# A gated delta rule layer: the triangular inverse started from 16x16 blocks that pass through memory, with a new order of steps

## The reference, cut to what matters

```python
q = silu(conv(x @ Wq)); k = silu(conv(x @ Wk)) * DK**-0.5; v = silu(conv(x @ Wv))   # causal, 4 taps
alpha = sigmoid(x @ Wa + ba); beta = sigmoid(x @ Wb + bb)
def step(S, inps):                      # scanned over the 2048 positions
    qt, kt, vt, at, bt = inps
    err = S @ kt - vt
    S = at * S - bt * outer(err, kt)
    return S, S @ qt
o = layernorm(o) * ln_w + ln_b
out = (o * sigmoid(x @ Wg)) @ Wo
```

## Time and profile before

| | |
|---|---|
| median of 3 runs | 3923.45 us |
| profiled execution, own time | 3925.09 us |
| its span (first to last instruction) | 3923.5 us |
| mean granted TensorE clock | 0.986 |
| TensorE busy | 3769.9 us, 96% |
| VectorE busy | 2704.0 us, 69% |
| ScalarE busy | 2204.4 us, 56% |
| GpSimd busy | 1281.8 us, 33% |
| DMA | 275.67 MB, 70 GB/s |

### The profile page before, as it was taken

The page is one execution under the profiler, slowest core; times in us unless marked ns, Lnnn a source line. Parts: engine busy times, 40 slices in busy tenths (PEclk is TensorE's granted clock), DMA queues, the critical chain, the costliest instruction groups (busy, mean ns, idle before and its releaser), DMA issues. The chain is left out here.

```text
span 3923.5 us, 119759 instructions
## 1 busy us (share of the span) xinstructions
PE 3769.9 (96%) x41088; PEld 3063.9 (78%) x41088; DVE 2704.0 (69%) x6942; ACT 2204.4 (56%) x6016; POOL 1281.8 (33%) x2594
## 2 busy tenths in 40 slices
PE   7999889999999999999999999999999999987999
PEld 5777668888888888888788888888888888866887
DVE  3444458878788777788777778777887878863222
ACT  3433356666666666666666666666666666652111
POOL 3434433333333333333333333333333333320000
PEclk9999989999999999999999999999999999988999
DMA  3343341111111211111321111111111211215443
GB/s 134 111 147 141 117 128 45 51 45 47 45 45 48 55 50 46 45 48 48 90 88 46 45 48 48 45 48 45 47 49 45 48 45 45 50 24 163 144 146 109
DMA packets 371786, 275.67 MB, mean 70 GB/s; under 512 B 153457, under 2 KB 284529, under 8 KB 369361
## 3 DMA queue, kind: packets, MB, share of 16 engines
q1 hardware_dynamic: 368848, 261.29, 23.5%
q0 software_dynamic: 2560, 8.39, 0.6%
HBM read 209.85 MB, written 59.77 MB: 69 GB/s over the span
## 5 line engine op out<-in xcount | busy, mean ns | idle before, releaser
L1084 DVE SCALAR_TENSOR_TENSOR conv<-bank,tap,conv 128x512 f32<-128x512 f32 x1152 | 857.6, 744 | 79.3 <-ACT conv L1233 56.4
L1295 PE MATMUL bank<-hx_hi,w_hi 128*128 128x512 f32 x2048 | 874.2, 427 | 35.2 <-POOL w_lo L913 24.0
L1295 PE MATMUL bank<-hx_hi,w_lo 128*128 128x512 f32 x2048 | 899.4, 439 | 0.0
L1295 PE MATMUL bank<-hx_lo,w_hi 128*128 128x512 f32 x2048 | 881.5, 430 | 0.0
L1295 PEld LDWEIGHTS bank<-hx_hi,w_hi 128*128 128x128 f32 x2048 | 391.3, 191 | 71.7 <-issue 49.0
L1295 PEld LDWEIGHTS bank<-hx_lo,w_hi 128*128 128x128 f32 x2048 | 389.0, 190 | 50.7
L931 POOL TENSOR_TENSOR prods<-Lb,Tc 128x28 f32<-128x28 f32 (+6 forms) x896 | 203.6, 227 | 683.6 <-ACT Lb L1219 621.2
L1295 PEld LDWEIGHTS bank<-hx_hi,w_lo 128*128 128x128 f32 x2048 | 389.9, 190 | 40.1
L965 POOL TENSOR_TENSOR oG<-oT,gT 128x512 f32<-128x512 f32 x128 | 163.7, 1279 | 721.7 <-ACT oT L1254 721.7
L1037 DVE SCALAR_TENSOR_TENSOR S<-S,gamma,bank 128x128 f32<-128x128 f32 x480 | 163.6, 341 | 203.9 <-PE bank L1376 191.7
L1207 ACT ACTIVATE Wc<-bank 128x128 f32<-128x128 f32 x512 | 141.4, 276 | 242.4 <-PE bank L1367 242.3
(11 more groups left out here) (156 smaller groups left out, 8836.3 us busy)
## 6 DMA issues: line engine op xcount, KB each, us to landing
gamma<-gamma_d SPq DMA_DIRECT2D x128, 258.0 KB, 3.4
alpha<-alpha_d SPq DMA_DIRECT2D x128, 256.0 KB, 3.1
oT_d<-oG SPq DMA_DIRECT2D x128, 256.0 KB, 2.4
o_raw<-oT_d SPq DMA_DIRECT2D x32, 1024.0 KB, 6.8
gu_raw<-in_gate_up SPq DMA_DIRECT2D x17, 1408.0 KB, 6.3
dn_raw<-in_down SPq DMA_DIRECT2D x17, 512.0 KB, 4.5
x_in<-in_x SPq DMA_DIRECT2D x8, 1024.0 KB, 9.3
w_raw<-in_Wk SPq DMA_DIRECT2D x32, 256.0 KB, 3.6
```

Of the source, the lines that this page charges most:

```text
L1084: dve.scalar_tensor_tensor(out=conv[i][:, to], in0=PJ[PJ_OF[(g + 3) % 4][i]][:], scalar=tap[:, i, j + 1:j + 2], in1=conv[i][:, to], op0=AL ...
L1295: last = pe.matmul(dst, a[:, i, k], b[:, k, cols], start=(j == 0), stop=(j == 3 * KC - 1))
```

## The change

- SB goes from 8 to 16: GpSimd inverts 16x16 diagonal blocks, 15 columns, so 30 instructions in place of 14. One doubling level of 32x32-block products (16 to 32) is left.
- The blocks reach GpSimd in another way. ScalarE copies four 32-partition diagonal blocks from LT into diag, GpSimd masks them and adds the two halves (Lc), SP stores Lc twice to a buffer in DRAM (32 KB each), waits, and loads it as Lb with one broadcast of 16 rows of 4 KB to 128 partitions (512 KB). The spreading matmul, Lx, the four products, the reduction and the copy of Lb go.
- TensorE visits the blocks twice a turn, in steps 20 and 1: each visit holds 16 products of 32x32, 8 between 32-row quarters and 4 of 64x64, of three successive groups.
- The stages are further apart: projections run one group further ahead, kT and gT have 6 buffers, qT, vT, decay and TT 3. There is a fourth ramp turn, and the last head has no projection at all. The loop body is three heads.
- For the first chunk of a head (S is zero) the two matmuls with S and R are left out, for the last chunk the one that would update S, and one k transpose in the third group.
- All tables of steps are new. On VectorE, T16 (the transpose of the solved blocks) and LT are both in step 18, T16 first. On SP, the stores and the load stand behind alpha, ahead of the weights and of oG's store. On GpSimd the next weight cut of a head's last turn stands in step 36, the start of the solve in step 37.
- At the start of the stage ScalarE cuts the first weights before it waits for the masks.

The diff, cut to its core:

```diff
-SB = 8
+SB = 16
 TB = 32
-LEVELS = [8, 16]
+NB = P // SB
 STEPS = 38
-
-CHAIN = {0: 0, 5: 1, 8: 2, 11: 3, 13: 4, 17: 5, 20: 6, 24: 7, 26: 8, 29: 9, 32: 10, 34: 11}
+UNROLL = 3
+
+CHAIN = {1: 0, 6: 1, 8: 2, 11: 3, 15: 4, 18: 5, 19: 6, 22: 7, 23: 8, 26: 9, 30: 10, 36: 11}
...
-A_AT, KT_AT, VT_AT, ON_TURN_AT, L_AT, BASE_AT = 1, 2, 11, 18, 24, 30
-VISIT_AT = {9: 0, 15: 1, 28: 2, 34: 3}
-SOLVE_AT = {34: (0, 2), 36: (2, 4), 0: (4, 6), 2: (6, 7)}
-T8P_AT, POW_AT, QG_AT, OG_AT = 4, 8, 17, 20
-AT_AT, K_AT, T8_AT, TN64_AT, DECAY_AT, LT_AT, DIAG_AT, LX_AT = 2, 3, 3, 21, 16, 25, 26, 28
-BN_AT, AGGR_AT, ON_AT = 1, 6, 9
-YB_AT = {11: 0, 28: 1}
-TT_AT = {19: 0, 31: 1}
-CONV_AT = {12: (0, 0), 14: (0, 1), 16: (0, 2), 20: (1, 0), 22: (1, 1), 25: (1, 2), 29: (2, 0), 33: (2, 1), 37: (2, 2)}
-VSILU_AT, GATE_AT, DIAGB_AT, VROWS_AT, KSILU_AT, QSILU_AT, OT_AT, LB_AT = 4, 5, 16, 11, 16, 25, 21, 28
-PLACE_AT = {8: (0, 1), 7: (2, 3)}
-TN_PLACE_AT = 23
-LATE_COPY = {8: 0, 17: 1, 27: 2, 37: 3}
-O_AT = {14: 0, 23: 1, 34: 2, 2: 3}
-TAP_AT = {11: 0, 20: 1, 25: 2}
-CUT_AT = {(0, 17): 0, (0, 21): 1, (0, 36): 2, (1, 4): 3}
-LATE_PER = 4
+A_AT, KT_AT, VT_AT, ON_TURN_AT, L_AT = 5, 2, 8, 22, 18
+VISIT_AT = {20: 0, 1: 1}
+SOLVE_AT = {37: (0, 1), 0: (1, 4), 1: (4, 6), 4: (6, 9), 7: (9, 11), 9: (11, 14), 11: (14, 15)}
+T16P_AT, POW_AT, QG_AT, OG_AT, DIAG_AT, LC_AT = 11, 15, 28, 29, 18, 17
+AT_AT, K_AT, T16_AT, TN64_AT, DECAY_AT, LT_AT = 6, 4, 18, 16, 7, 18
+BN_AT, AGGR_AT, ON_AT = 4, 5, 19
+YB_AT, TT_AT = 35, 0
+CONV_AT = {8: (0, 0), 9: (0, 1), 12: (0, 2), 19: (1, 0), 22: (1, 1), 23: (1, 2), 32: (2, 0), 33: (2, 1), 35: (2, 2)}
+VSILU_AT, GATE_AT, DIAGB_AT, VROWS_AT, KSILU_AT, QSILU_AT, OT_AT = 1, 16, 0, 14, 15, 30, 29
+PLACE_AT = {30: (0, 1), 7: (2, 3)}
+TN_PLACE_AT = 6
+MT32_AT, TT64_AT, MT64_AT, TT128_AT = 21, 4, 27, 6
+O_AT = {16: 0, 28: 1, 29: 2, 1: 3}
+TAP_AT = {14: 0, 17: 1, 28: 2}
+CUT_AT = {(3, 20): 0, (3, 23): 1, (3, 36): 2, (0, 18): 3}
 SOLVE_PER = 2 * (SB - 1)
-BUILT = 9 + 3 * len(LEVELS)
+BUILT = 12
...
-        diag = sb("diag", [P, G, TB])
-        Lc = sb("Lc", [P, G, SB])
-        Lx = sb("Lx", [P, G, SB, SB])
-        Lb = sb("Lb", [P, G, SB, SB])
+        Lb = sb("Lb", [P, SB, G, SB])
         prods = sb("prods", [P, G, SB])
+        Lc = prods
+        diag = same[:].rearrange("p (c t) -> p c t", t=TB)
...
+            turn(eng, -1, 0, 8, False, False, False, False, True, False)
+            turn(eng, -1, 1, 9, False, False, False, True, True, False)
+            turn(eng, -1, 2, 10, False, False, True, True, True, False)
+            turn(eng, -1, 3, 11, False, True, True, True, True, False)
             for g in range(GROUPS):
-                turn(eng, 0, g, True, True, True, True, g > 0)
-            with nc.Fori(1, NH - 1, engines=bass.OrderedEngineSet([eng.engine]), hint_back_edge=True) as hh:
-                for g in range(GROUPS):
-                    turn(eng, hh, g, True, True, True, True, True)
+                turn(eng, 0, g, g, True, True, True, True, True, g > 0)
+            with nc.Fori(1, NH - 1, UNROLL, engines=bass.OrderedEngineSet([eng.engine]), hint_back_edge=True) as h3:
+                for j in range(UNROLL):
+                    for g in range(GROUPS):
+                        turn(eng, h3 + j, g, (4 + 4 * j + g) % 12, True, True, True, True, True, True)
             for g in range(GROUPS):
-                turn(eng, NH - 1, g, True, g < 3, g < 2, g < 1, True)
-            turn(eng, NH, 0, False, False, False, False, True)
+                turn(eng, NH - 1, g, 4 + g, True, g < 3, g < 2, g < 1, False, True)
+            turn(eng, NH, 0, 8, False, False, False, False, False, True)
...
+            def spread(hh, g, d):
+                at = counter(hh, g)
+                for half in range(2):
+                    if half == 0:
+                        sp.wait_ge(lc_done, at(1, d + 1))
+                    sp.dma_start(base_d[:, half], Lc[:].rearrange("p c t -> p (c t)")).then_inc(base_stored, 16)
+                sp.wait_ge(base_stored, at(32, d + 1))
+                row = SB * G * SB
+                sp.dma_start(Lb[:].rearrange("p i c t -> p (i c t)"),
+                             bass.AP(base_d.tensor, 0, [[row, P // 8], [0, 8], [1, row]])).then_inc(base_loaded, 16)
...
+                if not (isinstance(hh, int) and hh == NH - 1):
+                    spread(hh, g, 4)
+                if g == 1 and after_next:
...
+                    if proj and s == LC_AT:
+
+                        pool.wait_ge(diag_done, at(4, 5))
+                        pool.tensor_tensor(diag, diag, same_c[:].rearrange("p (c t) -> p c t", c=1)
+                                           .to_broadcast([P, G, TB]), ALU.mult).then_inc(masked, 1)
+                        wait(pool, solve_done, at(SOLVE_PER, 4))
+                        pool.wait_ge(masked, at(1, 5))
+                        pool.tensor_tensor(Lc[:], diag[:, :, 0:SB], diag[:, :, SB:TB], ALU.add).then_inc(lc_done, 1)
+                    if inv and s == T16P_AT:
...
+                    if inv and s == T16_AT:
+
+                        dve.wait_ge(t16_done, at(1, 4))
+                        wait(dve, mid_done, at(2, 1, 1))
+                        wait(dve, tn_placed, at(2, 2))
+                        dve.transpose(Tnb[:, par], TTb[:, par]).then_inc(tn_done, 1)
...
+                    if proj and s == DIAG_AT:
+
+                        act.wait_ge(lt_done, at(1, 5))
+                        wait(act, masked, at(1, 4))
+                        for q in range(P // TB):
+                            act.activation(diag[quad(q)], LT[quad(q), g, :, quad(q)], ACT.Copy).then_inc(diag_done, 1)
...
-                    if proj and s == LB_AT:
-
-                        act.wait_ge(spread_done, at(1, 4))
-                        wait(act, t8_done, at(1, 3))
-                        act.activation(Lb[:].rearrange("p c t i -> p (c t i)"), TR[:, 0:G * SB * SB], ACT.Copy)\
-                           .then_inc(lb_done, 1)
...
                 def visit(v):
 
-                    if inv:
+                    if inv if v == 0 else mid:
...
+                    if mid if v == 0 else late:
...
+                    if late if v == 0 else chain:
...
+                    first, final = g == 0 and c == 0, g == 3 and c == 3
+                    if r == 0 and not first:
...
+                        if not first:
+                            pe.matmul(w[:, 3 * D:], q_gamma[:, cur, chunk(c)], S[:], start=True, stop=False)
+                        last = pe.matmul(w[:, 3 * D:], AT[:, cur, c], Wc[:], start=first, stop=True)
+                        if not final:
+                            last = pe.matmul(w[:, 2 * D:3 * D], k_rows[:, cur, c], Wc[:], start=True, stop=True)
+                        last.then_inc(chain_done, 1)
...
-                    if proj and s == BASE_AT:
-
-                        pe.wait_ge(lx_done, at(1, 4))
-                        pe.matmul(TR[:, 0:G * SB * SB], same[:], Lx[:].rearrange("p c t i -> p (c t i)"),
-                                  start=True, stop=True).then_inc(spread_done, 1)
```

More of the change, by code:

```diff
@@ L881, in _ @@
             n = 0
[L882 to L883 removed]
+            for tile in (none[:], TT[:], Tn64[:], decay[:, :, :, 0:1]):
                 pool.memset(tile, 0.0).then_inc(built, 1)
                 n += 1
+            pool.memset(oT[:, 0:P], 0.0).then_inc(built, 1)
             pool.memset(same[:], 1.0).then_inc(built, 1)
+            n += 2
+            pool.wait_ge(built, n)
+            part = oT[:, 0:P].rearrange("p (q r) -> p q r", r=TB)[:, :, 0:SB]
+            pool.memset(part, 1.0).then_inc(built, 1)
             n += 1
[L888 removed]
             blocks = same[:].rearrange("p (q r) -> p q r", r=SB)
@@ L894, in _ @@
                 pool.wait_ge(built, n)
+            for base, step, mult in ((-SB, -TB, 1), (TB - 1, TB, -1)):
+                pool.affine_select(out=part, in_=part, compare_op=ALU.is_ge, fill=0.0, base=base,
+                                   pattern=[[step, P // TB], [0, SB]], channel_multiplier=mult).then_inc(built, 1)
+                n += 1
+                pool.wait_ge(built, n)
             pool.wait_ge(sel_built, G)
@@ L916, in _, with turn @@
                 cut_low(i, i + 1)
-            pool.wait_ge(compact_built, 1 + len(LEVELS))
-            def turn(pool, hh, g, chain, late, inv, proj, ln):
+            pool.wait_ge(compact_built, 2)
+            def turn(pool, hh, g, n, chain, late, mid, inv, proj, ln):
                 at = counter(hh, g)
@@ new lines, in turn @@
+                    if late and s == MT64_AT:
+                        act.wait_ge(late_done, at(2, 1, 1))
+                        for odd in range(2):
+                            rows = slice(0, 64) if odd else slice(64, 128)
+                            act.activation(MT[64:128, odd::2], w64[rows], ACT.Copy).then_inc(mt64_done, 1)
+                    if chain and s == TT128_AT:
+                        act.wait_ge(late_done, at(2, 1))
```

(28 more changed lines are left out.)

462 lines of the change are left out of this document (205 added, 257 removed).

## The result

The changed kernel takes 3767.07 us (median of 4 runs, 3762.55 to 3769.11), the one before 3923.95 (4 runs beside it): ratio 0.9595, 95% interval 0.9579 to 0.9612, 157 us less. The prediction was 3711 us with a range of 3642 to 3835: right in sign and range, and 56 us too low.

A forecast was written before the change was run, and what follows sets the result against it. The prediction took TensorE as the bound before, and TensorE (21.4 us a turn) and the inverse's loop (20.6) as nearly level after. 1034.1 us plus 124 turns of 21.6 gave 3712.5, as median 3711, range 3642 to 3835.

The forecast's parts named there:

- The bound: Heads stage before the change: TensorE, busy 98%, sets the steady turn of 23.44 us; only its work or waits count.
- Parts 1 to 3: TensorE's small-block visits (0.94), spreading matmul (0.62), skipped chain steps (0.17): 1.73 to 2.2 us a turn saved, 2.0 taken.
- TensorE then needs 21.4 us a turn.: TensorE's turn in the heads stage after the savings: 21.4 us, between 21.2 and 21.7.
- Part 5: New loop through the inverse (T16, LT, stores, load, solve): 20.6 us, bounds 19.9 and 24.5; turn taken as 21.6.
- Scans against the solve: VectorE's four decay scans taking turns with GpSimd's solve would add 1.3 us, a loop of 21.9; scans above 0.42 speak for it.
- Part 6: Loop body of three heads, ten back edges for thirty: 16 us or 0.13 a turn saved, or nothing; inside the 21.6.
- Part 7: Start and end of the stage: +21 us (0 to 35) for the ramp, +18 for the fourth turn without projection.
- The sum: Whole kernel: T = 1034.1 + 124x us, x the turn; 21.6 gives 3712.5, the median of runs 3711.
- A: Inverse's loop alone decides, scans and solve in turn, late T16 on top: turn 22.4, 3812 us; chance 0.2.
- B: TensorE alone decides and its upper saving holds: turn 21.1, 3650 us; chance 0.12.
- C: Round trip through memory at its upper bounds, 9.8 us for 5.9: loop 24.5, 4072 us, slower than before; chance 0.07.
- D: New TensorE waits between second and third chunk's steps, now one apart, eat most savings: turn 23.0, 3886 us; chance 0.06.

The follow-up runs named there:

- no trip: Changed kernel without the stores, the 512 KB load and the wait for it, the solve working on zeros: 3720.18 us, ratio 0.948.
- load in two: Changed kernel with the broadcast load split into 128 KB and 384 KB, each with its own wait (also called the split kernel): 3745.09 us, ratio 0.9542.
- the last version: Changed kernel with third weight cut on VectorE, load in two pieces, other steps for the cuts and two ramp x loads issued later: 3685.95 us, ratio 0.9395.

## Why the prediction was right or wrong, step by step

- **The bound.** Right in the main: TensorE set the turn before and sets it after, but for two intervals of four in which the loop holds it by 0.5 and 0.1 us.
- **Parts 1 to 3, 2.0 us off TensorE.** Right in sum: the turns away from the head's change went from 23.14 to 21.15 (no trip, load in two), 1.99 less. The new visits take 1039.97 - 1038.64 - 0.31 = 1.02 us (0.95 predicted). The spread is worth 0.63, or 0.57 beside the unrolled loop (0.62). The skips 0.10 to 0.14 (0.17). The 0.31 that I took for a plain step is the one right behind other matmuls; behind another projection matmul it is 0.23 or 0.24 at most places of the same stretch. That makes each visit and the spread 0.08 dearer, so the sum of the parts would have been some 1.97 and not 1.73, an estimate from those rows. But the pieces don't add up as they were worked out: the passes of the dropped level, priced at 0.76, gave 0.1 to 0.2, and 0.29 on the mean, while the chain stood where it was.
- **"TensorE then needs 21.4 us a turn."** This is the term that was off. It took 2.0 from 23.44, a mean with 0.28 us of waits at the back edge in it, and so carried these over. After, the waits around the head's change are 0.60 a turn (21.75 - 21.15). Worked out from the split kernel's timeline over 27 heads, each between two matmul starts less the usual step: T16 behind the weight cut 0.73 us a head, two late Wc of 0.74 and 0.54, and before or at the first product of the new chain 0.63 for the copy of TT in 18 heads or 0.44 for issue in the nine with the back edge. These make 2.6 us a head, 0.65 a turn. Taken as 21.75, TensorE alone would have given T = 3731.
- **Part 5, the loop.** Half right. Its parts, means of the trace after (the 0.49 is that of the second interval, which waits for nothing else): T16 and the way to LT 0.26 at the least, LT to mask 2.10, mask and sum 0.86, to the load's issue 2.6, load 4.7, solve 10.2, T16P to T16 0.49: 21.2 us without a weight cut, where I had 20.3. The stores were 0.5 too low (the second starts 0.68 us behind the first, where I had 0.4) and the load 0.8 (4.6 to land, 3.8 predicted). So loop and TensorE are level, and what the trip costs the turn is 0.16 us, close to the 0.2 that I added. The weight cut I spread over the head as 0.3 of loop; it is a wait of TensorE's, 0.73 us a head or 0.18 a turn, trip or no trip, and moving it gave 0.5 to 0.6 a head.
- **Scans against the solve.** The solve took 10.2 us to T16P's start, and the sum without any taking of turns was 9.9. In the timeline a product beside a scan took 0.36 us between neighbours of 0.26 and 0.28. Over the trace, worked out by size, a solve instruction beside a scan is 0.02 us longer than one without, 0.1 us a turn. The scans have a median of 0.41 us (0.399 before); the one of 1.2 us is the very first, at 500.8, ahead of any solve, and no other took over 0.55. By the prediction's own sign, over 0.42, 213 of the 512 scans speak for the lock, but the size does not: 0.1 to 0.3 us a turn and not 1.3. By the rule of the Trainium skill, "SBUF — State Buffer", section "SBUF: two separate sides", the loop would have been 21.9. The trace does not agree: its whole solve is 0.3 us over the sum without it.

```profile
L1113 DVE TENSOR_TENSOR_SCAN decay<-alpha,diag_b x512: 383/410/1215, 500.8 to 3287.3; 128x128 f32<-128x128 f32 x171
```

- **Part 6.** Right: 0.14 us a turn in the kernel before by the table and 0.11 by the total (0.13 predicted), and 0.41 beside the turn without the spreading matmul.
- **Part 7.** 15 us too low. The constant is 3765.86 - 124 x 21.905 = 1050 where I had 1034.1. Three loops of the ramp take 72.4 us (30.6, 20.9, 20.9), not 60.9: the first waits in SyncE's queue. The rest, 4 us, is at the end. Two more misses of 7 to 8 us cancel: the first scan starts 8 us earlier than before (500.8), and the ways from it to the first LT and from the last loop to the chain are longer than the 3 and 7 that I had.
- **The sum.** 124 x (21.905 - 21.6) = 38 us and 15 us of the constant are 53 of the 56; the last 3 are the profiled execution against the median, 1.2 under it after, where I took it as 1.6 over it.
- **Rivals.** A (loop alone, 22.4) and C (trip 2.7 us over) fell: the trip is 1.3 over. B was nearly right that TensorE alone decides (the trip is worth 0.16 us a turn) and wrong in its 21.1: that is the turn without the head's change. D named the place, the third chunk's middle and last step one apart, but not the cause, which is ScalarE's weight cut ahead of Wc, and had five times its price (1.6 us a turn, the two late Wc are 0.32).

## What to carry to other kernels

Work out the turn from turns without a gap and the waits at the rare turn (a back edge, a change of head) apart, and look at what each edit does to either: a mean hides that the first fell by 2.0 and the second rose by 0.3. When the engine that sets the time gets faster, small instructions that stood ahead of its inputs on other engines (here 0.63 us and 1.28 us of weight cuts) become its waits, and moving them cost nothing here: together with a load in two pieces, the first small, and another order of loads in the ramp they gave 2.2% more. Taking out one of two nearly level limits shows little; the run without the trip told more than its total, by the turns that stayed.

## What was not expected of the hardware

- The wait for issue of TensorE's weight loads at the loop's back edge grew when its work shrank, from 0.8 us once a head to 2.1 (20.9 and 54.8 us at 26 places), and 94 us came of two edits that gave 54 singly.
- Issuing a 32 KB store of 128 rows takes SyncE 0.62 us, as long as the 512 KB load (0.57). The small beta load's issue, 0.38 at the median, took 2.43 behind megabyte loads.
- 512 KB land in 4.6 us; in two pieces 128 KB in 2.8 and the 384 KB behind them in 4.0, on the page of the last version:

```profile
Lb<-base_d SPq DMA_DIRECT2D x128, 384.0 KB, 4.0
...
Lb<-base_d SPq DMA_DIRECT2D x128, 128.0 KB, 2.8
```
